# Attention's turned outputs and maxima copied out of PSUM by ScalarE, outputs scaled by GpSimd, and expert weight pieces awaited one by one

## The reference

```python
# attention of a layer: q = layernorm(x), k = v = ctx (4, 512, 128); 32 query heads, 8 key heads, D = 16, G = 4
qh = q.reshape(b, s, KVH, G, D).transpose(0, 2, 3, 1, 4)
kh = k.reshape(b, s, KVH, D).transpose(0, 2, 1, 3)
vh = v.reshape(b, s, KVH, D).transpose(0, 2, 1, 3)
attn = softmax(einsum('bkgsd,bktd->bkgst', qh, kh) / sqrt(D), axis=-1)
out = einsum('bkgst,bktd->bkgsd', attn, vh)        # back to (b, s, 512)

x = x + tanh(g_xattn[0]) * attention0(layernorm(x), ctx, ctx)
x = x + tanh(g_ffn[0]) * moe0(layernorm(x))        # 8 experts, top 2, hidden 256, shared part 1024
x = x + tanh(g_xattn[1]) * attention1(layernorm(x), ctx, ctx)
x = x + tanh(g_ffn[1]) * moe1(layernorm(x))        # 32 experts, top 6, hidden 192, shared part 384
```

## Time and profile before

| what | value |
|---|---|
| median of three executions | 2183.56 us (2182.73 to 2184.03) |
| the profiled execution's own time | 2185.23 us |
| its span, first to last instruction | 2183.5 us |
| mean granted TensorE clock | 0.965 of full speed |
| TensorE matmul busy | 1980.4 us (91%) |
| VectorE busy | 1367.5 us (63%) |
| ScalarE busy | 1086.4 us (50%) |
| GpSimd busy | 715.1 us (33%) |

### The profile page before, as it was taken

The page is one execution under the profiler, slowest core; times in us unless marked ns, Lnnn a source line. Parts: engine busy times, 40 slices in busy tenths (PEclk is TensorE's granted clock), DMA queues, the critical chain, the costliest instruction groups (busy, mean ns, idle before and its releaser), DMA issues. The chain is left out here.

```text
span 2183.5 us, 40476 instructions
## 1 busy us (share of the span) xinstructions
PE 1980.4 (91%) x10072; PEld 1220.5 (56%) x10073; DVE 1367.5 (63%) x2675; ACT 1086.4 (50%) x1673; POOL 715.1 (33%) x848
## 2 busy tenths in 40 slices
PE   4999999979999999993899999988788999999997
PEld 2343333334567657882334333333556888888886
DVE  6898988832234324442889898874876455555553
ACT  1666666741212115541476666662212556666664
POOL 3111211111201005554111121120664555556654
PEclk9999999989999999996799999998999999999998
DMA  4422222151000127765332222204004889988996
GB/s 126 117 55 60 58 62 56 42 191 40 0 1 1 62 83 182 179 109 116 109 86 55 59 65 55 61 11 152 0 1 147 179 184 207 200 197 201 207 207 105
DMA packets 96016, 219.88 MB, mean 101 GB/s; under 512 B 16930, under 2 KB 20004, under 8 KB 95908
## 3 DMA queue, kind: packets, MB, share of 16 engines
q1 hardware_dynamic: 61540, 138.80, 21.6%
q0 software_dynamic: 33792, 79.71, 19.2%
q10 hardware_dynamic: 576, 0.00, 0.0%
HBM read 114.64 MB, written 56.63 MB: 78 GB/s over the span
## 5 line engine op out<-in xcount | busy, mean ns | idle before, releaser
L567 DVE TENSOR_REDUCE maxima<-ring_ps 128x1 f32<-128x512 f32 x1024 | 647.7, 683 | 96.0 <-PE ring_ps L378 95.7
L464 ACT ACTIVATE probs<-score_ps 128x1024 f32<-128x1024 f32 x512 | 503.7, 1025 | 210.6 <-PE score_ps L395 208.8
L378 PE MATMUL ring_ps<-k_turned,q_turned 64*128 64x512 f32 x1024 | 412.5, 481 | 57.9 <-DVE maxima L567 20.3
L378 PEld LDWEIGHTS ring_ps<-k_turned,q_turned 64*128 64x128 f32 x1024 | 176.5, 192 | 374.1 <-DVE maxima L567 232.6
L1077 PE MATMUL bank_f<-w_gu_parts_f,xg_T_f 128*128 x1800 | 368.4, 353 | 1.6 <-issue 1.6
L1077 PEld LDWEIGHTS bank_f<-w_gu_parts_f,xg_T_f 128*128 128x128 f32 x1800 | 327.1, 190 | 30.0 <-issue 2.2
L395 PE MATMUL score_ps<-q_turned,k_turned 64*128 64x512 f32 x1024 | 331.3, 446 | 12.9 <-ACT probs L464 12.8
L410 PE MATMUL out_ps<-probs,v_ones 128*32 128x512 f32 x2048 | 274.5, 608 | 1.8 <-ACT probs L464 1.6
L1102 PE MATMUL bank_f<-w_dn_parts_f,hg_T_f 96*128 (+1 forms) x888 | 243.8, 410 | 2.6 <-DVE hg_T_f L1638 1.4
L902 POOL DMA_INDIRECT out_x<-y_tok_f,idx_out_f x111 | 177.4, 1598 | 139.5 <-ACT y_tok_f L1276 109.7
L886 POOL DMA_INDIRECT xg_f<-xh_rows_f,idx_in_f x156 | 159.8, 1025 | 183.3 <-DVE idx_in_f L1528 118.4
(11 more groups left out here) (210 smaller groups left out, 2213.1 us busy)
## 6 DMA issues: line engine op xcount, KB each, us to landing
w_gu_f<-in_L_w_gu SPq DMA_DIRECT2D x64, 384.0 KB
q_turned<-q_hi SPq DMA_DIRECT2D x128, 128.0 KB, 2.6
w_dn_f<-in_L_w_dn SPq DMA_DIRECT2D x32, 384.0 KB
k_turned<-k_hi SPq DMA_DIRECT2D x128, 64.0 KB, 2.1
q_turned<-no_max SPq DMA_DIRECT2D x64, 128.0 KB, 2.6
q_turned<-q_lo SPq DMA_DIRECT2D x64, 128.0 KB, 2.6
xh_rows_f<-xh_f SPq DMA_DIRECT2D x8, 1024.0 KB, 9.0
w_gu_f<-in_L_w_gu SPq DMA_DIRECT2D x16, 512.0 KB
```

The costliest lines, as they stand in the source:

```text
L378: pe.matmul(ring(k, "max", i), q_turned[rows, slot, h // 2, c * P:(c + 1) * P], k_turned[rows, slot, :], start=True, stop=True).then_inc(m ...
L464: act.activation(probs[:, c % 2, pair, :, :], score_ps[:, pair, :, :], ACT.Exp, scale=float(D) ** -0.5).then_inc(exped, 1)
L567: dve.tensor_reduce(maxima[:, par, col:col + 1], ring(k, "max", i), AX.X, ALU.max).then_inc(max_taken, 1)
```

## The change

In attention, three pieces of work move between engines. `copy_max` moves from VectorE to ScalarE. The turned outputs are first copied whole (128x272) by ScalarE into a new SBUF tile `turned_out`; the bank is then free. The inversion stays on VectorE, but reads the copy, after reduce n = 8. The multiplication moves to GpSimd, in front of its addition. ScalarE's two copies stand behind exp 3 of the step.

`next_batch` starts its statistics a step later: k = 2 the four `bn_stats`, k = 3 the aggregation at n = 0 and `split_k` at n = 4 and 8; `normalize` stays in k = 4, and `root` moves to k = 3.

With the experts, each load waits only for the split of the piece that it overwrites, and each `gu_hi` only for its own piece.

```diff
-TURN_AT, TURN_Q_AT, SCALE_AT = 2, 5, 6
-COPY_OUT_AT, COPY_Q_AT = 1, 6
+TURN_AT, TURN_Q_AT, INVERT_AT = 2, 5, 8
+COPY_OUT_AT, COPY_TURN_AT, COPY_Q_AT = 1, 3, 6
...
             # GpSimd, add_x
-                pool.wait_ge(out_read, u + 1)
+                rows = turned_out[:].rearrange("p (n e) -> p n e", n=SLOTS)
+                pool.wait_ge(recip_ready, u + 1)
+                if u >= 1:
+                    pool.wait_ge(x_added, u)
+                pool.nop(nofuse=True)
+                pool.tensor_tensor(out=scaled[:], in0=rows[:, :, 0:D], in1=recip[:, :, None].to_broadcast([P, SLOTS, D]),
+                                   op=ALU.mult).then_inc(out_scaled, 1)
+                pool.wait_ge(out_scaled, u + 1)
...
-                if k == 2 and b < B - 1:
+                if k == 3 and b < B - 1:
                     root(b + 1)
...
             # ScalarE
+            def copy_turned(b, k):
+                if (u := stage(b, k, LAG_OUT)) is None:
+                    return
+                act.wait_ge(out_turned, u + 1)
+                if u >= 1:
+                    act.wait_ge(out_scaled, u)
+                act.activation(turned_out[:], ring(k, "turn")[:, 0:SLOTS * USED], ACT.Copy).then_inc(out_read, 1)
+
+            def copy_max(b, k):
...
+                act.wait_ge(max_turned, u + 1)
+                if past(b, k, LAG_NEG + 2):
+                    act.wait_ge(max_placed[par], 16 * u + (0 if par == 0 else -16))
+                act.activation(max_rows[:, par, :], ring(k, "turn")[0:2 * SLOTS, SLOTS * USED:SLOTS * USED + P], ACT.Copy
+                               ).then_inc(max_copied, 1)
...
+                    if n == COPY_TURN_AT:
+                        copy_turned(b, k)
+                        copy_max(b, k)
...
             # VectorE
-                if k == 1:
+                if k == 2:
                     if c == 0:
                         dve.wait_ge(x_loaded[b + 1], 16)
                     moments_of_tile(b + 1, c)
-                elif k == 2 and c == 0:
+                elif k == 3 and c == 0:
                     moments_of_batch(b + 1)
-                elif k == 3 and c < 2:
-                    split_k(b + 1, c)
+                elif k == 3 and c < TPB - 1:
+                    split_k(b + 1, c - 1)
...
+            def invert_sums(b, k):
                 if (u := stage(b, k, LAG_OUT)) is None:
                     return
...
+                dve.wait_ge(out_read, u + 1)
+                if u >= 1:
+                    dve.wait_ge(out_scaled, u)
+                dve.reciprocal(recip[:], turned_out[:].rearrange("p (n e) -> p n e", n=SLOTS)[:, :, D]).then_inc(recip_ready, 1)
...
-                    if n == SCALE_AT:
-                        copy_max(b, k)
-                        scale_out(b, k)
+                    if n == INVERT_AT:
+                        invert_sums(b, k)
...
             # SyncE, experts
                 for piece in range(2):
+                    if not isinstance(e, int):
+                        sp.wait_ge(gu_split, 2 * e + (piece - 3))
+                        sp.nop(nofuse=True)
...
+                if not isinstance(e, int):
+                    sp.wait_ge(dn_split, e - 1)
+                    sp.nop(nofuse=True)
...
                     sp.wait_ge(expert_w, 48 * e)
                     sp.nop(nofuse=True)
-                    sp.wait_ge(gu_split, 2 * e - 2)
-                    sp.nop(nofuse=True)
-                    sp.wait_ge(dn_split, e - 1)
-                    sp.nop(nofuse=True)
...
             # ScalarE, experts
-                act.wait_ge(expert_w, 48 * e + 48)
+                act.wait_ge(expert_w, 48 * e + (16 * piece + 16))
...
             def dn_hi(e):
+                act.wait_ge(expert_w, 48 * e + 48)
```

More of the change, by code:

```diff
@@ L83, in make_attention @@
         out_rows = sb("out_rows", [P, S])
-        recip = sb("recip", [P, SLOTS])
+        recip, turned_out = sb("recip", [P, SLOTS]), sb("turned_out", [P, SLOTS * USED])
         scaled = sb("scaled", [P, SLOTS, D])
@@ L100, in make_attention @@
         out_copied, out_turned, picked = sem("out_copied"), sem("out_turned"), sem("picked")
+        out_scaled = sem("out_scaled")
         recip_ready, out_read, x_added = sem("recip_ready"), sem("out_read"), sem("x_added")
@@ L455, in copy_q @@
                 act.activation(q_raw[:, (k + 3) // 2 % 2, :], ring(k, "q"), ACT.Copy).then_inc(q_copied, 1)
+            def copy_turned(b, k):
[6 more added lines that the diff above has]
+            def copy_max(b, k):
+                if (u := stage(b, k, LAG_NEG)) is None:
+                    return
+                par = (k - LAG_NEG) % 2
+                act.wait_ge(max_turned, u + 1)
[3 more added lines that the diff above has]
+                               ).then_inc(max_copied, 1)
             def exp(b, k, c, pair):
@@ L567, in take_max @@
                 dve.tensor_reduce(maxima[:, par, col:col + 1], ring(k, "max", i), AX.X, ALU.max).then_inc(max_taken, 1)
-            def copy_max(b, k):
-                if (u := stage(b, k, LAG_NEG)) is None:
-                    return
-                par = (k - LAG_NEG) % 2
-                dve.wait_ge(max_turned, u + 1)
-                if (out := stage(b, k, LAG_OUT)) is not None:
-                    dve.wait_ge(out_turned, out + 1)
-                if past(b, k, LAG_NEG + 2):
-                    dve.wait_ge(max_placed[par], 16 * u + (0 if par == 0 else -16))
-                dve.tensor_copy(max_rows[:, par, :], ring(k, "turn")[0:2 * SLOTS, SLOTS * USED:SLOTS * USED + P]
-                                ).then_inc(max_copied, 1)
-            def scale_out(b, k):
+            def invert_sums(b, k):
                 if (u := stage(b, k, LAG_OUT)) is None:
                     return
-                turned_out = ring(k, "turn")[:, 0:SLOTS * USED].rearrange("p (n e) -> p n e", n=SLOTS)
-                dve.wait_ge(out_turned, u + 1)
-                dve.reciprocal(recip[:], turned_out[:, :, D]).then_inc(recip_ready, 1)
-                dve.wait_ge(recip_ready, u + 1)
-                if past(b, k, LAG_OUT + 1):
-                    dve.wait_ge(x_added, u + 0)
-                dve.tensor_tensor(scaled[:], turned_out[:, :, 0:D],
-                                  recip[:, :, None].to_broadcast([P, SLOTS, D]), ALU.mult).then_inc(out_read, 1)
+                dve.wait_ge(out_read, u + 1)
+                if u >= 1:
+                    dve.wait_ge(out_scaled, u)
+                dve.reciprocal(recip[:], turned_out[:].rearrange("p (n e) -> p n e", n=SLOTS)[:, :, D]).then_inc(recip_ready, 1)
             def step(b, k):
```

## The result

The changed kernel takes 2155.88 us (median of four runs, 2151.34 to 2160.62) beside 2183.8 us for the kernel before in the same comparison (four runs, 2182.73 to 2187.91): ratio 0.9864, 95% interval 0.9835 to 0.9894. The profiled execution took 2151.34 us (span 2149.6), 33.9 less than the profiled one of before. This execution was the fastest of its four, so 28 is the gain to carry and 33.9 the one that the trace can divide.

What follows compares the result with a forecast made beforehand. The handshake of TensorE and VectorE over three ring banks bounds attention. Terms of -5.8 a layer, -11.6 for both, and -1 for the experts took the profiled 2185.2 to 2172.6, so 2171 us by the median; forecast range 2164 to 2178.

Steps and rivals of the forecast that it cites:

- What binds a turn round: Attention's turn rounds: VectorE's work on the bank holds TensorE; without it a clean round lasts 3.39 for 3.84, gaining 0.44.
- ScalarE's copies: In attention: copies of 272 and 128 columns take 0.39 and 0.26, hold ScalarE's queue 0.49, hidden by 0.76 idle.
- The tie with exponential 4: Attention, behind the copies: exponential 4 ends at 366.42 and TensorE wants it at 366.45, a margin of 0.03.
- the rival of the other side: Attention: ScalarE's wait comes on the path if copies and wake-ups exceed 0.49; 2178 to 2192 us, chance 0.17.
- 46x: Attention, both layers: loss in clean and draining rounds if copies and wake-ups take x more than 0.49.
- GpSimd: Attention: the multiplication takes 0.73 there, as its addition; split_max ends at 172.1, wanted about 174.0, so nothing is late.
- Statistics in the second and third batch: Attention: turn rounds of k=1, k=2, k=3 last 3.39, 4.19, about 4.3; later rounds of k=2 lose 0.45 and 0.35.
- the steady part: Attention 0, from round 1 of step 3 up to the draining steps: -8.4 us.
- The ends: Each attention layer: draining steps +1.0 from held exponential 4, very end +0.7 from copy, multiplication and wait in series.
- First batch, statistics in k = 2 with nothing to gain: +0.9: Each attention layer: moving the first batch's statistics to k = 2 gains nothing and costs 0.9 us.
- more gain: Attention: 0.44 had in all 58 rounds, 25 us, and experts up to 5; 2155 to 2164 us, chance 0.13.
- the experts: Expert weight loads: starting them earlier saves little, -1 us, with bounds of +3 and -5.

Runs made afterwards that it cites:

- experiment 2: Kernel before with ScalarE's two copies and GpSimd's multiplication alone, statistics and expert waits as before: 2164.67 us, ratio 0.9899.
- experiment 6: Changed kernel with two extra 128x128 ScalarE copies per step behind the copy of the maxima: 2165.76 us, ratio 0.990.
- experiment 11: Changed kernel with the multiplication back on VectorE, at n = 8 behind the inversion, reading the SBUF copy: 2166.04 us, ratio 0.9906.
- experiment 4: Changed kernel with ScalarE's two copies behind exponential 4 instead of 3: 2154.2 us, ratio 0.9841.
- experiment 1: Kernel before with the statistics, split_k and root a step later, and nothing else of the change: 2177.08 us, ratio 0.9946.
- experiment 5: Kernel before with batch 1's x loaded in SyncE's prologue, no VectorE work moved: 2177.18 us, ratio 0.9948.
- experiment 3: Kernel before with the expert loads' and splits' waits by piece alone: 2180.72 us, ratio 0.9963.
- experiment 8: Kernel before with ScalarE waiting only for its own piece of expert weights, SyncE loading as before: 2183.98 us, ratio 0.9988.
- experiment 7: Changed kernel with ScalarE's copies behind exponential 4 and, for batches 2 and 3, statistics and K's division in odd steps: 2147.24 us, ratio 0.9817.
- experiment 10: Kernel of experiment 7 with batch 1's x loaded in the prologue and the first batch's statistics in step 1: 2146.99 us, ratio 0.9811.

## Why the prediction was right, and where it was wrong

**What binds a turn round: right.** The forecast put a clean one at 2.40 + 0.99 = 3.39; it is 3.40 in every clean step. The release by VectorE was the hold, and experiment 2 has its worth, 10.1 us from first to last addition.

**ScalarE's copies: right in price, slack mis-sized.** Forecast 0.39 and 0.26, and 0.49 for both in the queue. The source views of the two lines, after (count, then ns min/median/max):

```profile
L471 ACT ACTIVATE turned_out<-ring_ps x64: 397/397/398, 66.7 to 1430.5; 128x272 f32<-128x272 f32 x64
```

```profile
L481 ACT ACTIVATE max_rows<-ring_ps x64: 250/252/266, 39.2 to 1414.3; 32x128 fp32r<-32x128 f32 x64
```

They hold the queue from 203.15 to 203.60, 0.45. Idle ahead of them: 1.85 for a forecast of 1.7 to 1.8. The tie with exponential 4 had 0.09 us to spare where the forecast had 0.03. But a late exponential 4 is not paid in full, as the rival of the other side had it: 0.40 late cost 10.4 over both layers, not the 18 of its 46x, since TensorE waits for VectorE in the same round (experiment 6). The forecast had used this wait for exponential 5 and not in the rival.

**GpSimd: right.** The multiplication took less than forecast, and the additions have the times of the earlier trace rows:

```profile
L281 POOL TENSOR_TENSOR scaled<-turned_out,recip x64: 618/622/714, 69.9 to 1431.4; 128x256 f32<-128x256 f32 x64
```

```profile
L285 POOL TENSOR_TENSOR x_res<-x_res,scaled x64: 721/731/749, 70.8 to 1432.1; 128x256 f32<-128x256 f32 x64
```

The Trainium skill, page "Perfetto Trace Analysis", section "Optimizing Scalar/DVE Operations", warned of the SBUF read port that VectorE and GpSimd share. The medians, 731 ns beside 733 before, show no slowing, and experiment 11, which put the multiplication back on VectorE, was the slower. But the 714 above is not chance. Six of the 64 multiplications took 686 to 714 ns, and they are those that began while VectorE ran a `normalize` (L538); the 58 others took 618 to 637, and those beside a `bn_stats`, which reads SBUF as well, 619 to 622. Changed kernel, VectorE and GpSimd:

```profile
169.82 0.46 DVE L538 TENSOR_SCALAR xh<-x_res,mean_var,rstd 128x512 f32<-128x512 f32 x1
...
170.07 0.69 POOL L281 TENSOR_TENSOR scaled<-turned_out,recip 128x256 f32<-128x256 f32 x1 [6.22 <-DVE recip L605]
```

In experiment 11 the additions fell there, and six of them took 897 to 904 ns where the median is 737. So the two engines do slow each other here, beside one instruction and three times a layer, by less than 0.2 us each. That is too little to be seen in the time, and that the shared port is its reason is not shown by these runs.

**Statistics in the second and third batch: near, and somewhat dear.** Forecast for k = 1, 2 and 3: 3.39, 4.19 and 4.3, and 0.45 and 0.35 in the two rounds behind k = 2's second. The table has 3.40, 4.18, 4.08, and 0.31 and 0.28. For k = 3 the sign was wrong, since it fell from 4.19 to 4.08, and the turn round of k = 4, which the forecast left as it was, fell from 4.06 to 3.89. These make most of the 1.1 us by which the steady part gained more than its 8.4.

**The ends: right**, +1.7 forecast and +1.7 measured in attention 0, of which experiment 4 takes 1.0 back.

**The failed step: "First batch, statistics in k = 2 with nothing to gain: +0.9."** The forecast priced the move of the first batch's statistics as VectorE work alone and left out what they waited for. The move ended a wait of 4.91 us for batch 1's x, behind which the reduces and TensorE stood. In place of +0.9 it gave -6.2 us in attention 0 and, by the same sum, about -5.9 in attention 1 (-13.68 + 9.5 - 1.7). That is 14 of the 21.3 us by which the profiled difference missed the sum. Experiments 1 and 5 show the cause by two different edits. The window of the earlier trace rows begins at 60 us, and the single rounds all lay in the steady stage. The trace of the kernel before had the wait ahead of that: from 20 to 40 us TensorE was busy for 11.0 us, and VectorE's row at 30.54, shown above, names the transfer.

```profile
20.00:40.00 20.00, 11.03 (x22) 5.00 (x22) 11.61 (x19) 0.56 (x2) 3.41 (x2) 1.00 0.53 161
```

No rival covered it. The measured 2155.88 lies in the range that "more gain" was given, 2155 to 2164, by luck: that rival had 25 us from the turn rounds alone, and the steady parts gave 9.5 in each layer.

**A term mis-sized: the experts.** Forecast -1. Experiment 3 gives -0.4% beside its own group's kernel before, some 8 us, and 3 us beside the 2183.8 of the first comparison; the profiles give no more than a hint, in the next paragraph. So the size of this term stays open.

**The rest of the profiled 33.9 us is at least in part the draw of two executions.** The tiles of layer 0, -2.7: TensorE's loads and matmuls waited 2.8 and 2.4 us for gathers before, and 1.3 and 1.1 after. Kernels without any edit to the experts can have the short value too (experiment 2: 188.68, experiment 5: 188.77) or the long one (before: 191.25, experiment 1: 190.8), as can experiment 8 with ScalarE's half (191.56). But all eight profiled kernels whose SyncE loads by piece have the short one, 188.4 to 189.0. Whether the earlier load takes away the long case, or eight draws fell that way, is not shown. Routing and shared expert of layer 1, -2.9 with the same 124 matmuls; the windows of before, then of after:

```profile
1480.57:1532.03 51.46, 44.07 (x124) 18.58 (x124) 27.93 (x79) 15.11 (x25) 3.82 (x4) 0.90 0.35 121
```

```profile
1449.28:1497.74 48.46, 40.88 (x124) 17.77 (x124) 27.69 (x79) 15.11 (x25) 3.83 (x4) 0.96 0.37 128
```

The third number from the right is the granted clock, 0.90 and 0.96; the counts of instructions are the same. Experiment 5, which touches nothing there, had the short stretch as well (209.22), so this one needs no part of the change. With these 5.6 us taken out, 28.3 are left, near the 27.9 between the medians of the first comparison.

## What to carry to other kernels

Read the fill of a pipeline on its own. An instruction moved a step later there may cost nothing and end a wait that the steady stage never shows, so look up the first instance of every moved instruction and what it waited for, on its own engine's row: the engine that suffers names only its neighbour.

Work that frees a shared bank belongs on the engine that idles when the bank is filled, and work that can be anywhere belongs in the rounds where its engine waits for another (here rounds 2 and 3 of odd steps). When two queues tie within a tenth of a microsecond, a dummy copy measures the real slack, and the rows behind it tell which other wait shares it.

## What the runs showed of the hardware

A GpSimd multiplication of 128x256 by a broadcast 128x16 took 622 ns where an addition of two full 128x256 tiles took 731. VectorE's multiplication of 128x256 had a median of 425 ns from PSUM before (the earlier trace rows has one of them) and of 425 from SBUF in experiment 11: the source made no difference.

The fill of attention can differ by 2.6 us between two executions of the same attention code, by TensorE's clock alone. The kernel before took 52.67 us from attention 1's first reduction to its first addition, and experiment 3, whose attention is the same, 55.27. In the 25 us up to step 3's turn round both had a granted clock of 0.50, the lower level of 1.2 GHz, with TensorE busy 22.06 us in both. Then the clock rose in one and not in the other. The windows of rounds 1 and 2 of step 3, before and then experiment 3; the third number from the right is the granted clock:

```profile
1068.34:1075.04 6.70, 5.77 (x38) 2.13 (x34) 5.45 (x10) 3.08 (x3) 0.00 (x0) 0.98 0.54 194
```

```profile
1063.28:1072.59 9.31, 9.17 (x37) 3.22 (x33) 5.85 (x10) 3.07 (x3) 0.00 (x0) 0.51 0.47 161
```

The same two rounds took 6.70 and 9.31 us, and a max score 0.50 and 0.79. Of the 2.9 us between experiments 7 and 10 in the same fill (51.02 and 48.13) 2.6 have this cause too: those two rounds took 9.20 us in layer 1 of experiment 7 and 6.60 in its layer 0, with the same work. The late rise of experiment 4 in layer 0 is the third case. There the clock column of the windows reads 1.00 (so it does at the start of every kernel here) though the matmuls take 0.79, so at the start of a trace it is the matmul's own duration that tells the level.
